# A two-layer graph kernel: the fourth pair of attention probabilities goes through DRAM too, and the steps are reordered

## The chip, the cores and the metric

One core of a Trainium2 chip. The metric is device time in microseconds (us), the median of three runs. Times inside a run are read from one profiled execution. Engines are named as the profile names them: PE is TensorE (PEld its weight loads), DVE is VectorE, ACT is ScalarE, POOL is GpSimd, SP is SyncE, whose queue issues every DMA here.

## The reference, cut to what matters

```python
# x: (64, 256, 512) f32; adj: (256, 256) 0/1
x = layernorm(x + deg*(x @ Wi.T + b) + adj @ (x @ Wj.T))            # layer 0
q, k, v = heads(x @ Wq.T + bq), heads(x @ Wk.T + bk), heads(x @ Wv.T + bv)   # 8 heads of 64
scores = where(adj == 0, -inf, q @ k.T / 8)                          # 256 x 256 for each head
out = layernorm(x + (softmax(scores) @ v) @ Wo.T + bo)               # layer 1
```

## The kernel before

The 64 graphs (batches) run one after the other, software-pipelined by hand. `steps` issues 63 steps and a `last_step`. Step b does, for batch b, scores, softmax and attention; for batch n = b + 1 the first layer and q, k, v; for batch b - 1 the output projection `y` and the last layer norm. Every product is made of three f32 products of split operands (`_hi` and `_lo` parts), so each operand costs a copy for the high part and a subtraction for the low part. The 8 heads are 4 pairs (`g` = 0 to 3, two heads `i` in each).

Every engine has its own instruction list, written out by hand in `step`, and runs it strictly in order; semaphores tie the lists together. So an instruction that waits holds back all that is listed behind it on its engine. SP's list is such a list too: a DMA whose semaphore is late holds back the DMAs behind it.

The path of one pair's probabilities: PE makes `scores` into two of the four `attn` banks; DVE `maxima_of_head` adds the mask, writes `probs` and the row minima; ACT `exponentials`; DVE `inverse_sums`; ACT `normalise_even` and POOL `normalise_odd` scale the two heads. The product with v needs them transposed. Before the change pair 0 is transposed by PE (`transpose_p`, 8 transposes of 128x128 into PSUM, L675), copied by ACT (`pt_high`) and split by DVE (`pt_low`). Pairs 1 to 3 are transposed in 32x32 blocks by DVE (`flip`, L1074) and the blocks are moved to their places by SP (`move`): one DMA of 512 KB `bounce<-probs` (L280), a wait for its landing, then four DMAs of 128 KB `pT_raw<-bounce` (L285). ACT `p_high` and DVE or POOL `p_low` split them, and PE `attend` uses them.

`probs` has two slots, g % 2. So the maxima of pair 2 may be written only when pair 0 has left slot 0, and those of pair 3 when pair 1 has left slot 1. Before, the maxima of pair 2 wait for PE's transposes (`pt_done`), those of pair 3 for `moved[1]`. Pairs run in the order 1, 0, 2, 3 (function `at`).

In each step SP's list is: `load_x` (L271), `load_xT` (512 KB, L268, which waits until PE has finished the last product of the first layer, `l0_done`), the three moves, and the store of batch b - 1.

The last layer norm is applied on DVE (`norm_apply`, L1145, two instructions of 128x512 a step).

## Time and profile before

| | |
|---|---|
| median of 3 runs | 2925.93 us (2925.61 to 2926.91) |
| the profiled execution's own time | 2926.99 us |
| its span, first to last instruction | 2925.2 us |
| PE busy | 2845.6 us, 97% |
| DVE, ACT, POOL busy | 2258.0, 1871.2, 1883.9 us |
| mean granted clock of PE | 0.996 of full |
| DMA share of 16 engines, hardware queue | 32.1% |

A step of the steady loop takes 44.80 us, so the 63 steps are nearly the whole span. Matmuls are pipelined, and their shown durations overlap: what one costs is the distance from its start to the next start. The same holds for DVE and ACT.

### The profile page before, as it was taken

What the parts mean: (1) busy time and instruction counts of PE and PEld (TensorE: products, weight loads), DVE (VectorE), ACT (ScalarE), POOL (GpSimd) and SP (SyncE); (2) the same over time, 40 slices, a digit from 0 to 9 for tenths busy, and PEclk for the clock granted to TensorE, in tenths of its full rate; (3) what the DMA queues carried; (4) which work ended last, traced back from release to release, by engine and by line L of the source; (5) the groups of instructions that cost most, each with busy time, mean ns of one, the idle gap of its engine ahead of it and who ended that gap; (6) DMA issues with size and microseconds to landing.
All of it is one profiled execution on the core that took longest, in us unless ns stands there. A gap on an engine that the chain in (4) does not pass through costs nothing.

```text
span 2925.2 us, 59805 instructions
## 1 busy us (share of the span) xinstructions
PE 2845.6 (97%) x18584; PEld 2457.2 (84%) x18584; DVE 2258.0 (77%) x5774; ACT 1871.2 (64%) x4874; POOL 1883.9 (64%) x1794
## 2 busy tenths in 40 slices
PE   6999999999999999999999999999999999999997
PEld 5888888888888888888888888888888888888886
DVE  7687777777877877778778777777787787777776
ACT  4666666666666666666666666666666666666665
POOL 5667666576676675665766766657667667666573
PEclk9999999999999999999999999999999999999999
DMA  4333333333333333333233333333333332333321
GB/s 137 109 102 102 115 100 108 108 98 111 107 100 112 103 100 110 105 108 105 96 115 102 104 110 103 105 108 103 112 101 100 115 100 100 115 100 108 107 92 60
DMA packets 282405, 306.72 MB, mean 105 GB/s; under 512 B 18817, under 2 KB 214913, under 8 KB 282369
## 3 DMA queue, kind: packets, MB, share of 16 engines
q1 hardware_dynamic: 282368, 306.26, 32.1%
q8 instruction: 19, 0.31, 0.0%
q14 instruction: 18, 0.14, 0.0%
HBM read 173.55 MB, written 132.64 MB: 105 GB/s over the span
## 4 chain that ended last, share of the span: by engine, by line
POOL 36%; issue 31%; PE 23%; DVE 7%; POOLq 1%; ACT 0%; DMA 0%; DVEq 0%; SPq 0%
PE proj L535 12%; POOL pT_lo L400 10%; POOL xb L395 5%; PE proj L498 4%; POOL probs L391 4%; POOL xs_lo L368 3%; PE attn L660 3%; POOL oT_lo L423 3%; DVE hb L1145 3%; POOL hb L409 3%; POOL mj_lo L379 2%; PE av L498 2%; POOL xs_raw L352 2%; POOL xs_raw L349 1%; DVE pT_lo L1078 1%
## 5 line engine op out<-in xcount | busy, mean ns | idle before, releaser
L400 POOL TENSOR_TENSOR pT_lo<-pT_raw,pT_hi 128x512 fp32r<-128x512 f32 x315 | 403.3, 1297 | 402.7 <-ACT pT_hi L856 402.7
L825 ACT ACTIVATE probs<-probs,row_min 128x256 f32<-128x256 f32 x1024 | 509.0, 499 | 225.5 <-DVE row_min L1043 222.9
L391 POOL TENSOR_TENSOR probs<-probs,row_inv 128x512 f32<-128x512 f32 x256 | 266.9, 1043 | 434.1 <-DVE row_inv L1054 434.1
L1043 DVE CUSTOM_DVE_ANT_0 probs<-attn,mask_add 128x256 f32<-128x256 f32 x1024 | 375.9, 418 | 41.8 <-PE attn L660 39.8
L862 ACT COPY o_part<-av 64x512 f32<-64x512 f32 x256 | 149.6, 584 | 395.1 <-PE av L498 389.1
L535 PE MATMUL proj<-wji_hi,xs_hi 128*128 128x512 f32 x896 | 363.4, 406 | 14.7 <-DVE wji_lo L1222 10.8
L535 PE MATMUL proj<-wji_hi,xs_lo 128*128 128x512 f32 x896 | 355.6, 397 | 0.0
L535 PE MATMUL proj<-wji_lo,xs_hi 128*128 128x512 f32 x896 | 355.6, 397 | 0.0
L1074 DVE STREAM_TRANSPOSE probs<-probs 128x1024 f32<-128x1024 f32 x189 | 234.7, 1242 | 114.5 <-PE av L498 114.5
L616 PE MATMUL proj<-mj_hi,wq_hi 128*128 128x256 f32 x1024 | 293.4, 286 | 11.3 <-DVE mj_lo L997 11.3
L1145 DVE TENSOR_SCALAR hb<-hb,mean_var_out,rstd_out 128x512 f32<-128x512 f32 x128 | 156.4, 1261 | 188.1 <-POOL rstd_out L418 188.0
L368 POOL TENSOR_TENSOR xs_lo<-xs_raw,xs_hi 128x768 fp32r<-128x768 f32 x126 | 295.9, 2349 | 0.2
L616 PE MATMUL proj<-mj_hi,wq_lo 128*128 128x256 f32 x1024 | 288.6, 282 | 0.0
L616 PE MATMUL proj<-mj_lo,wq_hi 128*128 128x256 f32 x1024 | 288.2, 281 | 0.0
L498 PE MATMUL av<-pT_hi,v_both 128*128 128x256 f32 x1016 | 258.7, 287 | 30.0 <-DVE pT_lo L1078 25.9
L498 PE MATMUL proj<-mj_hi,wk_lo 128*128 128x256 f32 x1024 | 287.7, 281 | 0.0
L498 PE MATMUL proj<-mj_hi,wk_hi 128*128 128x256 f32 x1024 | 287.6, 281 | 0.0
L498 PE MATMUL proj<-mj_lo,wk_hi 128*128 128x256 f32 x1024 | 287.3, 281 | 0.0
L1088 DVE SCALAR_TENSOR_TENSOR oT<-av,bv_cols,o_part 64x256 f32<-64x256 f32 x512 | 242.9, 474 | 17.0 <-ACT o_part L862 13.4
L834 ACT ACTIVATE probs<-probs,row_inv 128x256 f32<-128x256 f32 x512 | 232.1, 501 | 36.0 <-DVE row_inv L1054 36.0
L498 PE MATMUL av<-pT_lo,v_both 128*128 128x256 f32 x1016 | 252.3, 282 | 0.0
L498 PEld LDWEIGHTS av<-pT_hi,v_both 128*128 128x128 f32 x1016 | 191.2, 188 | 62.8 <-issue 53.0
(126 smaller groups left out, 8611.2 us busy)
## 6 DMA issues: line engine op xcount, KB each, us to landing
bounce<-probs SPq DMA_DIRECT2D x189, 512.0 KB, 2.6
pT_raw<-bounce SPq DMA_DIRECT2D x756, 128.0 KB, 3.0
xs_raw<-in_xT SPq DMA_DIRECT2D x64, 512.0 KB, 4.1
xb<-in_x SPq DMA_DIRECT2D x64, 512.0 KB, 3.4
out<-hb SPq DMA_DIRECT2D x64, 512.0 KB, 2.8
w_raw<-in_w0T SPq DMA_DIRECT2D x8, 256.0 KB, 5.6
stage<-in_wqT SPq DMA_DIRECT2D x1, 1024.0 KB, 10.6
stage<-in_wkT SPq DMA_DIRECT2D x1, 1024.0 KB, 12.5
```

The source lines that it names most:

```text
L368: pool.tensor_tensor(xs_lo[:, blocks, :, :], xs_raw[:, blocks, :, :], xs_hi[:, blocks.start - 1:blocks.stop - 1, :, :].bitcast(F32), ALU.s ...
L391: pool.tensor_tensor(e, e, inv, ALU.mult).then_inc(norm_odd_done, 1)
L400: pool.tensor_tensor(pT_lo[:, g % 2, :, :, i, :, :], pT_raw[:, g % 2, :, :, i, :, :], pT_hi[:, :, :, i, :, :].bitcast(F32), ALU.subtract). ...
L498: return pe.matmul(dst, lhsT, rhs, start=start, stop=stop)
L535: last = pe.matmul(proj[bank_][:, :], a[:, c, :], w[:, c, :, :].rearrange("p k o -> p (k o)"), start=(start and j == 0), stop=(j == len(te ...
L616: last = pe.matmul(dst[:, c, :], w[:, kk, cols], h[:, kk, :], start=(part == 0 and c == 0 and kk == 0 and j == 0), stop=(part == 1 and kk ...
L825: last = nc.scalar.activation(e, e, ACT.Exp, bias=row_min[:, g % 2, s:s + 1], scale=-1.0, accum_out=row_sum[:, g % 2, s:s + 1])
L834: last = nc.scalar.activation(e, e, ACT.Copy, scale=row_inv[:, g % 2, r:r + 1])
L1043: last = V.tensor_tensor_reduce(out=out_, in0=in_, in1=mask_, scale=1.0, scalar=MIN_CEILING, op0=ALU.add, op1=ALU.min, accum_out=row_min[: ...
L1074: V.transpose(both, both).then_inc(flip_done, 1)
L1088: last = V.scalar_tensor_tensor(out=oT[i * HALF:(i + 1) * HALF, g, :], in0=av[0:HALF, i * N:(i + 1) * N], scalar=bv_cols[:, 2 * g + i:2 * ...
L1145: V.tensor_scalar(row(r), row(r), mean_var[which][:, r, 0:1], rstd[which][:, r:r + 1], ALU.subtract, ALU.mult).then_inc(normed[which], 1)
```

## The change

- Pair 0 takes the path of the others: `flip`, `move`, `p_high`, `p_low`. PE's `transpose_p`, ACT's `pt_high` and DVE's `pt_low` remain only in `last_step`.
- `at` is gone: the pairs run 0, 1, 2, 3.
- The maxima of pair 2 wait for `bounced[0]`, those of pair 3 for `bounced[1]` (the landing of the DMA out of `probs`), those of pairs 0 and 1 for `bounced[2]` and `bounced[3]` of the step before.
- The last layer norm is applied on ACT (`norm_out`), from a shift that one small DVE instruction computes (`norm_shift`).
- The lists of PE, ACT, DVE and POOL are written in new orders. SP's list gets `move(b, 0)` ahead of `move(b, 1)`.

```diff
@@ SP
             def move(b, g):
-                sp.wait_ge(flip_done, 3 * b + g)
+                sp.wait_ge(flip_done, G * b + g + 1)
...
                     load_x(b + 2, parity)
                     load_xT(b + 2)
+                move(b, 0)
                 move(b, 1)
                 move(b, 2)
                 move(b, 3)
@@ PE, step
                 first_layer(n, U4)
-                transpose_p(b, 0, 0)
-                transpose_p(b, 0, 1)
                 scores(b, 1, only=2)
+                scores(b, 1, only=3)
                 aggregate(n)
                 if y_: y(b - 1, 0)
                 if y_: y(b - 1, 1)
+                transpose_h(n, 0, 1 - parity)
+                transpose_h(n, 1, 1 - parity)
                 attend(b, 0, not y_)
-                transpose_h(n, 0, 1 - parity)
-                scores(b, 1, only=3)
-                transpose_h(n, 1, 1 - parity)
                 q(n, 0)
                 q(n, 1)
                 attend(b, 1)
@@ ACT, new function
+            def norm_out(n, parity):
+                act.wait_ge(shift_done, n + 1)
+                for r in range(R):
+                    nc.scalar.activation(hb[:, parity, r, :], hb[:, parity, r, :], ACT.Identity, bias=shift[:, r:r + 1],
+                                         scale=rstd["out"][:, r:r + 1]).then_inc(normed["out"], 1)
@@ DVE, maxima_of_head
-                elif i == 0 and (g == 2 or tail and g == 3):
-
-                    dve.wait_ge(pt_done, 2 * b + 2 * (g - 2) + 2)
-                elif i == 0 and g == 3:
-
-                    dve.wait_ge(moved[1], 64 * (b + 1))
+                elif i == 0 and g >= 2:
+
+                    dve.wait_ge(bounced[g - 2], 16 * (b + 1))
+                elif i == 0 and not first:
+
+                    dve.wait_ge(bounced[g + 2], 16 * b)
@@ DVE, step, middle part
-                pt_low(b, 0, 0)
                 agg_sum(n, 1, other)
                 norm_stats("h", n, 0, read["agg"], h_row[other])
-                inverse_sums(b, 2)
                 norm_stats("h", n, 1, read["agg"], h_row[other])
                 norm_mean("h", n)
-                pt_low(b, 0, 1)
                 if y_: y_sum(b - 1, 0, other)
+                inverse_sums(b, 2)
+                maxima_of_head(b, 3, 0)
                 norm_apply("h", n, h_row[other])
+                p_low(b, 0, 0)
                 if y_: y_sum(b - 1, 1, other)
+                maxima_of_head(b, 3, 1)
+                hT_low(n, 0)
+                hT_low(n, 1)
                 flip(b, 2)
-                hT_low(n, 0)
-                maxima_of_head(b, 3, 0)
-                hT_low(n, 1)
...
-                if y_: norm_apply("out", b - 1, hb_row[other])
+                p_low(b, 2, 1)
+                if y_: norm_shift(b - 1)
                 o_sum(b, 2)
                 p_low(b, 3, 1)
@@ POOL, step
+                normalise_odd(b, 0)
                 if y_: split_o(b - 1, 3)
+                mj_low(n, 0)
                 normalise_odd(b, 1)
-                normalise_odd(b, 0)
-                mj_low(n, 0)
                mj_low(n, 1)
```

Three places in the lists, as the built programs have them. On DVE, from the flip that stands among the sums of the first layer (`mj_lo` and `xb<-proj,deg,xb` are those sums; `row_min` marks the maxima, `xb<-proj,xb` the sum of the aggregation). Before:

```order
L1074 STREAM_TRANSPOSE probs<-probs 128x1024 [waits norm_odd_done,norm_even_done,av_done]
L1106 TENSOR_TENSOR mj_lo<-proj,mj_hi 128x256 [waits mj_hi_done,l0_done]
L1114 SCALAR_TENSOR_TENSOR xb<-proj,deg,xb 128x256
L1043 ISA probs,row_min<-attn,mask_add 128x8x32 [waits score_done,pt_done]
L1043 ISA row_min 128x1
```

After:

```order
L1072 STREAM_TRANSPOSE probs<-probs 128x1024 [waits norm_odd_done,norm_even_done,av_done]
L1054 RECIPROCAL row_inv<-row_sum 128x4 [waits exp_done]
L1104 TENSOR_TENSOR mj_lo<-proj,mj_hi 128x256 [waits mj_hi_done,l0_done]
L1112 SCALAR_TENSOR_TENSOR xb<-proj,deg,xb 128x256
L1072 STREAM_TRANSPOSE probs<-probs 128x1024 [waits norm_odd_done,norm_even_done,av_done]
L1043 ISA probs,row_min<-attn,mask_add 128x8x32 [waits score_done,bounced0]
L1043 ISA row_min 128x1
```

Pair 0 is flipped at the place where pair 1 was, pair 1 follows, and the maxima of pair 2 stand behind both with a wait for a DMA. Further down DVE's list, from the applied first layer norm (`xb<-xb,mean_var_h,rstd_h`) to the low part of its transpose (`mj_lo<-proj,mj_hi 128x512`, which PE's q waits for). Before:

```order
L1145 TENSOR_SCALAR xb<-xb,mean_var_h,rstd_h 128x512 [waits rstd_h_done]
L1145 TENSOR_SCALAR xb<-xb,mean_var_h,rstd_h 128x512
L1126 TENSOR_TENSOR hb<-proj,hb 128x512 [waits hb_ready,y_done]
L1074 STREAM_TRANSPOSE probs<-probs 128x1024 [waits norm_odd_done,norm_even_done,av_done]
L997 TENSOR_TENSOR mj_lo<-proj,mj_hi 128x512 [waits hT_hi_done]
```

After, from the maxima of pair 3:

```order
L1043 ISA probs,row_min<-attn,mask_add 128x8x32 [waits score_done,bounced1]
L1043 ISA row_min 128x1
L1043 ISA probs,row_min<-attn,mask_add 128x8x32
L1043 ISA row_min 128x1
L1152 TENSOR_SCALAR xb<-xb,mean_var_h,rstd_h 128x512 [waits rstd_h_done]
L1152 TENSOR_SCALAR xb<-xb,mean_var_h,rstd_h 128x512
L1076 TENSOR_TENSOR pT_lo<-pT_raw,pT_hi 128x8x64 [waits p_hi_done]
L1124 TENSOR_TENSOR hb<-proj,hb 128x512 [waits hb_ready,y_done]
L1043 ISA probs,row_min<-attn,mask_add 128x8x32 [waits score_done]
```

The maxima of pair 3 and their wait now stand ahead of the applied norm, and four more instructions stand between it and the low part. On SP, from the load of the transposed x. Before:

```order
L268 DMA xs_raw<-in_xT 128x1024 [waits l0_done]
L280 DMA bounce<-probs 128x1024 [waits flip_done]
L285 DMA pT_raw<-bounce 32x8x128 [waits bounced1]
L285 DMA pT_raw<-bounce 32x8x128 x3
L280 DMA bounce<-probs 128x1024 [waits flip_done]
L285 DMA pT_raw<-bounce 32x8x128 [waits bounced2]
```

After:

```order
L267 DMA xs_raw<-in_xT 128x1024 [waits l0_done]
L279 DMA bounce<-probs 128x1024 [waits flip_done]
L284 DMA pT_raw<-bounce 32x8x128 [waits bounced0]
L284 DMA pT_raw<-bounce 32x8x128 x3
L279 DMA bounce<-probs 128x1024 [waits flip_done]
L284 DMA pT_raw<-bounce 32x8x128 [waits bounced1]
```

The DMA out of pair 1's slot is now the second one, behind the four DMAs of pair 0.

## Rows read from the trace of the kernel before

**Rows 1.** The page: span, busy time by engine, one group of section 5.

```profile
span 2925.2 us, 59805 instructions
...
PE 2845.6 (97%) x18584; PEld 2457.2 (84%) x18584; DVE 2258.0 (77%) x5774; ACT 1871.2 (64%) x4874; POOL 1883.9 (64%) x1794
...
L1145 DVE TENSOR_SCALAR hb<-hb,mean_var_out,rstd_out 128x512 f32<-128x512 f32 x128 | 156.4, 1261 | 188.1 <-POOL rstd_out L418 188.0
```

**Rows 2.** Windows, one step: us; busy PE, PEld, DVE, ACT, POOL; PEclk; DMA; GB/s.

```profile
1405.26:1450.06 44.80, 44.21 (x293) 38.25 (x292) 34.83 (x89) 29.02 (x76) 29.39 (x29) 1.00 0.32 105
```

**Rows 3.** Waits of TensorE, whole span: total us, times, longest us.

```profile
PE av L498 <- DVE pT_lo L1078: 25.9, 63, 0.4
PE proj L616 <- DVE mj_lo L997: 11.3, 63, 0.6
...
PE proj L588 <- DVE xb L1145: 5.1, 1, 5.1
```

**Rows 4.** Timeline, TensorE, that step: start us, us, engine, line, operation, count, [idle].

```profile
1405.26 0.39 PE L660 MATMUL attn<-k_hi,q_hi 64*128 64x256 f32 x2
...
1406.88 0.50 PE L535 MATMUL proj<-wji_hi,xs_hi 128*128 128x512 f32 x1
...
1416.78 1.03 PE L675 MATMUL attn<-ident,probs 128*128 128x128 f32 x8
1417.74 0.39 PE L660 MATMUL attn<-k_hi,q_hi 64*128 64x256 f32 x2
...
1418.65 0.73 PE L498 MATMUL proj<-mj_hi,aT 128*128 128x512 f32 x2
...
1429.42 0.36 PE L616 MATMUL proj<-mj_hi,wq_hi 128*128 128x256 f32 x1 [0.17 <-DVE mj_lo L997]
```


**Rows 5.** The same timeline, the end of that step.

```profile
1450.06 0.39 PE L660 MATMUL attn<-k_hi,q_hi 64*128 64x256 f32 x2
```

**Rows 6.** Timeline of SyncE's queue, the same step.

```profile
1416.97 0.36 SPq L268 DMA_DIRECT2D xs_raw<-in_xT  x1
1417.57 0.34 SPq L280 DMA_DIRECT2D bounce<-probs  x1
1422.26 2.55 SPq L285 DMA_DIRECT2D pT_raw<-bounce  x4
1428.63 0.34 SPq L280 DMA_DIRECT2D bounce<-probs  x1
1431.27 2.54 SPq L285 DMA_DIRECT2D pT_raw<-bounce  x4
```

**Rows 7.** Timeline of SyncE's queue, a step that loads no x.

```profile
2850.33 0.33 SPq L280 DMA_DIRECT2D bounce<-probs  x1
2852.97 2.54 SPq L285 DMA_DIRECT2D pT_raw<-bounce  x4
```

**Rows 8.** Timeline of VectorE, the same step as rows 4.

```profile
1416.31 1.24 DVE L1074 STREAM_TRANSPOSE probs<-probs 128x1024 f32<-128x1024 f32 x1
...
1424.66 0.68 DVE L1126 TENSOR_TENSOR hb<-proj,hb 128x512 f32<-128x512 f32 x1
1425.33 1.00 DVE L1145 TENSOR_SCALAR xb<-xb,mean_var_h,rstd_h 128x512 f32<-128x512 f32 x2
1426.41 0.69 DVE L1126 TENSOR_TENSOR hb<-proj,hb 128x512 f32<-128x512 f32 x1
...
1428.58 0.69 DVE L997 TENSOR_TENSOR mj_lo<-proj,mj_hi 128x512 fp32r<-128x512 f32 x1
1429.19 0.41 DVE L1043 CUSTOM_DVE_ANT_0 probs<-attn,mask_add 128x256 f32<-128x256 f32 x1
...
1429.90 0.69 DVE L997 TENSOR_TENSOR mj_lo<-proj,mj_hi 128x512 fp32r<-128x512 f32 x1
...
1447.51 1.26 DVE L1078 TENSOR_TENSOR pT_lo<-pT_raw,pT_hi 128x512 fp32r<-128x512 f32 x1
```

**Rows 9.** Windows as rows 2, a stretch of the first step.

```profile
80.00:86.00 6.00, 5.36 (x29) 4.84 (x30) 4.14 (x9) 1.17 (x2) 0.97 (x3) 0.50 0.49 162
```

More of the change, by code:

```diff
@@ L215, in build @@
         flip_done, p_hi_done = sem("flip_done"), sem("p_hi_done")
-        moved = {g: sem(f"moved{g}") for g in (1, 2, 3)}
-        bounced = {g: sem(f"bounced{g}") for g in (1, 2, 3)}
-        p_split = {g: sem(f"p_split{g}") for g in (1, 2, 3)}
+        moved = [sem(f"moved{g}") for g in range(G)]
+        bounced = [sem(f"bounced{g}") for g in range(G)]
+        p_split = [sem(f"p_split{g}") for g in range(G)]
         stats_done = {k: sem(f"stats_{k}_done") for k in ("h", "out")}
@@ L640, in scores @@
                 pe.wait_ge(read["k"], 2 * b + pair + 1)
-                pairs = ((only,) if only is not None else (0, 1) if last else (1, 0))
+                pairs = (0, 1) if only is None else (only,)
                 if tail:
-                    pe.wait_ge(pt_read, 2 * b + 2 * (only - 2) + 2)
+                    pe.wait_ge(pt_read, 2 * (only - 2) + 2)
                 elif pair == 0 and not first:
                     pe.wait_ge(max_done, 2 * G * b)
-                elif only == 2:
-                    pe.wait_ge(max_done, 2 * (G * b + at(0)) + 2)
-                elif only == 3:
-                    pe.wait_ge(pt_read, 2 * b + 2)
+                elif only is not None:
+                    pe.wait_ge(max_done, 2 * (G * b + only - 2) + 2)
                 for g in pairs:
@@ L1136, in norm_mean @@
             def norm_mean(which, n):
+                if which == "out" and not (type(n) is int and n == 0):
+                    dve.wait_ge(normed["out"], R * n)
+                    dve.nop(nofuse=True)
                 dve.wait_ge(stats_done[which], R * n + R)
@@ L1325, in last_step @@
                 maxima(b, 3, tail=True)
+                o_sum(b, 1)
+                pt_low(b, 2, 0)
+                pt_low(b, 2, 1)
                 inverse_sums(b, 3, tail=True)
[L1327 to L1330 removed]
                 norm_mean("out", b - 1)
                 o_sum(b, 2)
[L1333 removed]
+                pt_low(b, 3, 0)
+                pt_low(b, 3, 1)
+                norm_shift(b - 1)
                 o_sum(b, 3)
[L1335 removed]
             steps(dve, step, last_step)
```

210 lines of the change are left out of this document (103 added, 107 removed).

## The prediction

> **What bounds the kernel now.** The page first: PE is busy for 97% of the span [rows 1]. Then one step of the loop, cut out as a window from the start of one `scores` to the next: 44.80 us, with PE at work for 44.21, DVE for 34.83, ACT for 29.02, POOL for 29.39, the clock at 1.00 and the DMA engines at 0.32 [rows 2]. Then the waits of PE: over the whole span it waits only in two places of the loop, 25.9 us for the low part of the last pair and 11.3 us for the low part of `hT`, 0.6 us a step together [rows 3]. So PE's own list is the bound, and the other engines have spare time in the mean. Spare time in the mean is not enough, though. Every other list is in order, and the chain that feeds PE's `q` may become later than PE. So I follow one step, on a clock that is 0 at the start of its first scores, 1405.26 in the trace. On that clock, before: the first layer starts at 1.62, the transposes at 11.52, scores of pair 2 at 12.48, the aggregation at 13.39, `q` at 24.16, and the next step at 44.80 [rows 4, 5]. From the start of `q` to the end of the step are 20.64 us.
>
> **What PE saves.** The 8 transposes occupy 11.52 to 12.48, 0.96 us. Two pairs of scores in one go take 1.62 us (0 to 1.62), one pair alone 0.91 us (12.48 to 13.39), so that putting pairs 2 and 3 together saves 2 x 0.91 - 1.62 = 0.20 us. Together 1.16 us a step, 73 us over 63 steps. The wait for the last pair's low part stays: it hangs on `p_high(b, 3)`, which waits for `attend(b, 2)`, as before.
>
> **What the other engines gain and lose.** DVE loses the second layer norm (2 x 1.26 us [rows 1]) and two `pt_low` (0.7 each, estimated from the equal shape of `mj_lo`, 0.69), and gains a flip (1.24) and two `p_low` (1.26 each) [rows 8]: 3.9 out, 3.8 in, so its 34.83 us stay. ACT gains two applications of 128x512. The rows have no such instruction on it; between nothing and DVE's 1.26 I take the high end, 2.5 us, which its 15.8 idle us a step hide, since the store that waits for them is needed only a step later. If that cover were gone it would cost up to 2.5. POOL has the same work in another order; its `mj_low(n, 1)` now waits behind `normalise_odd(b, 1)` and comes some 0.5 us late for the aggregation, which is swallowed by the larger wait below. DMA traffic of the moves rises by a third, from a share of 0.32 of the whole: room enough. None of this decides.
>
> **The new waits.** DVE's flip among the sums of the first layer starts at 11.05 and takes 1.24, so it is done at 12.3, just where SP issues the first bounce (12.31) [rows 6, 8]. After the change the same set of DVE work (four maxima, two `v_low`, one `o_sum`, the sums) stands ahead of that flip, so `flip(b, 0)` is done at the same time. Nor could an earlier one help: SP must first issue `xs_raw<-in_xT`, which waits for the end of the first layer and goes out at 11.71 [rows 6]. From there:
>
> 1. The first bounce is issued at 12.31 and the four DMAs behind its landing start at 17.00: 4.69 us, not the 2.63 us that a bounce takes later in the step (23.37 to 26.01) [rows 6]. The reason is the x load 0.60 us ahead of it: in a step without that load the first bounce takes 2.64 us [rows 7]. The maxima of pair 2, which before waited for PE's transposes, now wait for this landing. DVE stands still from about 14.7 (the first flip's end at 12.3, a sum of some 0.8 and a second flip of 1.24, with a short wait between) to 17.0, and the aggregation's sums, which free PE's bank for the second half of `y`, stand behind it.
> 2. SP needs 2.55 us to issue the four DMAs of pair 0 [rows 6], so that the bounce of pair 1, though flipped at 14.7, goes out at 19.6.
> 3. How long that bounce takes behind four DMAs of 128 KB, the trace doesn't show. Alone it is 2.63, behind 512 KB issued 0.6 us earlier 4.69. The four are the same 512 KB, but issued over 2.55 us, so most of it has moved by then: I take 3.3, nearer to the low end. It lands at 22.9.
> 4. The maxima of pair 3 wait for it, and behind them in DVE's list stand: head 0 of those maxima 0.71, the applied norm of the first layer 1.08, `p_low(b, 0, 0)` 1.26, `y_sum` 0.67, head 1 of the maxima 0.71, `hT_low` 0.69 (each as the distance between starts, or the duration, in [rows 8]), and 0.15 from the end of that to the start of `q` (1429.27 to 1429.42 [rows 4, 8]). Sum 5.27 us.
>
> So `q` starts at 22.9 + 5.27 = 28.2 in place of 24.16, 4.0 us late, although PE has less to do ahead of it. What is late next is the whole rest of the step: with 20.64 us behind it the step becomes 48.8 us. PE's waits then lie ahead of `transpose_h` (from about 22 to 24.7), and ahead of `q` (about 1 us), since `transpose_h` and `attend(b, 0)` are short.
>
> Is anything else late in the 20.64? Pair 1's reloads are issued by 25.5 and, with a landing as long as a bounce's, are there at 28.1. ACT reaches `p_high(b, 1)` only at about 30, after the exponentials of pair 3, and POOL's two halves, which I take as long as DVE's `p_low`, end at some 33.1. `attend(b, 1)` is due behind `q`, whose 48 products take some 5.8 us, at 33.9 or so. These three are estimates by the counting above. That is close but holds. Pairs 2 and 3 have more room.
>
> **The sum.** 61 full steps x 4.0 = 244 us. The step that loads no x gets its first bounce 2.05 us sooner: 2.0. The first step, which has no `y` and already waits 5.1 us for the applied norm [rows 3], I put at 3. The last step keeps PE's transposes: nothing. Together 249 us on the profiled execution's own 2926.99 us, which is 1.1 us above the median: 3176 us. With step 3 at its two ends (2.63 and 4.69) the step is 48.1 or 50.2 us, and the time 3135 or 3262: this case's own range.
>
> Of the bounce behind other DMAs the Trainium skill says (DMA: Bandwidth & Descriptors, Queues, rings and completion order) that each DMA engine takes its descriptors in ring order. By that rule the second bounce would move nothing until pair 0's reloads are through, nearer to 3.8 us than to 3.3, and the sum would be some 30 us more. The trace agrees in so far as the bounce behind the x load takes 2.05 us more than the one alone.
>
> **The rivals.**
>
> *The clock falls in the new waits.* Once in the trace PE waits 5.1 us, in the first step and for this same applied norm, and right behind it the granted clock is 0.50 from 80 to 86 us [rows 3, 9]; such a stretch of at least 6 us costs half its work, 3 us. In the changed steps PE would stand some 2.7 us and then 1 us. That is less than 5.1 at one go, so it needn't fall, and it may fall in some steps only. If it falls in a third of them: 21 x 3 = 63 us more, 3240 us; in all of them 3365 us. The Trainium skill (TensorE: Matmul & The Clock Gate, Why this matters for your kernels) warns of idle gaps of PE between bursts for this reason. By that rule the slower figures are the likelier ones; the trace shows only the one long wait.
>
> *The DMAs don't hold each other up.* If both bounces took 2.63 us, pair 0 would land at 14.95 and pair 1 at 20.2. `q` would start at 25.5, 1.3 us late, and the kernel would take 2927 + 63 x 1.3 = 3009 us. Against it stands that 4.69 us is what each step with an x load shows.
>
> *The other side: faster.* DVE's chain behind the second bounce needs 5.27 us and `q` must start by 24.16, so the change breaks even if that bounce lands by 18.9, and wins if it lands earlier. With no new wait at all PE's saving remains: 2927 - 73 = 2854 us. For it speaks that PE is the only engine near full [rows 2]. Against it, the bounce isn't issued before 19.6 by rows 6. It would need SP to issue the reloads faster, or a first bounce that doesn't feel the x load, and both together.
>
> **How the numbers follow.** Chances: the chain as worked out, clock up, 0.48; the same with the clock falling in some steps, 0.33 (0.04 of it above 3290); the milder one 0.09; the faster one 0.07; and 0.03 for a time within 0.2% (about 6 us, what a measurement of this kernel can tell from no change), where savings and waits cancel by chance. The likeliest gives 3176 us. The range from 3080 to 3290 leaves out the milder, the faster and the worst clock cases, 0.2 together or a little more. Faster 0.07, same 0.03, slower 0.90.
>
> **What would show it in the profile after.** In SP's queue: the first bounce 4.7 us ahead of its four reloads, the second bounce right behind them, and about 3.3 us to its landing. In the waits: DVE's maxima (L1043) waiting some 2 us a step for `bounce`, and PE waiting for `xb` ahead of `transpose_h` and for `mj_lo` ahead of `q`, 3 to 4 us a step together, where before it waited 0.2. The step at 48.8 us. PE's busy time down by some 60 us or more. The clock column in the windows behind those waits tells the first rival. The prediction is wrong if the first bounce lands by 15, or if DVE reaches the first flip much sooner than 11 and that turns out to matter, or if another engine's list (POOL behind pair 1's low parts is the closest) ends later than `attend(b, 1)`.

## The result, and the profile after

The changed kernel takes 3358.74 us (median of 4 runs, 3356.73 to 3359.12), the one before 2926.42 beside it: a ratio of 1.1476, 95% interval 1.1456 to 1.1496. That is 432 us slower, and 69 us above the upper end of the forecast range. The page after, to be read against [rows 1]:

```profile
span 3357.3 us, 59354 instructions
PE 2924.1 (87%) x18080; PEld 2481.4 (74%) x18080; DVE 2393.1 (71%) x5774; ACT 1966.4 (59%) x5000; POOL 1939.6 (58%) x1794
```

PE no longer fills its span. Its busy time did not fall by the transposes' worth; it rose by 78 us, and part of it ran at half clock (mean clock 0.958 of full, before 0.996). What PE waits for (against [rows 3]; total us, times, longest):

```profile
PE proj L588 <- DVE xb L1152: 251.4, 64, 10.0
PE av L498 <- DVE pT_lo L1076: 85.8, 63, 1.4
PE proj L498 <- DVE xb L1118: 49.1, 61, 1.0
```

And what DVE waits for. The first row is pair 2's maxima standing for the landing of pair 0's DMA to DRAM. The second names no releaser; in the step below it is pair 3's maxima, which start 0.10 us behind the issue of the reloads that wait for pair 1's landing:

```profile
DVE probs L1043 <- DMA bounce<-probs: 161.4, 63, 2.8
...
DVE probs L1043 <- issue: 81.0, 63, 2.0
```

The step of after that is read here starts at 1041.48 and lasts 51.58 us (the mean over all steps is 51.65, before 44.78). SP's queue in it (start, us), to be read against [rows 6]:

```profile
1053.39 0.35 SPq L267 DMA_DIRECT2D xs_raw<-in_xT  x1
1053.88 0.34 SPq L279 DMA_DIRECT2D bounce<-probs  x1
1058.86 2.56 SPq L284 DMA_DIRECT2D pT_raw<-bounce  x4
1061.53 0.53 SPq L279 DMA_DIRECT2D bounce<-probs  x1
1065.03 2.53 SPq L284 DMA_DIRECT2D pT_raw<-bounce  x4
```

The first trip takes 4.98 us, the second, behind the four reloads, 3.50. DVE and POOL behind the second landing (against [rows 8]):

```profile
1052.54 1.24 DVE L1072 STREAM_TRANSPOSE probs<-probs 128x1024 f32<-128x1024 f32 x1
...
1058.98 0.42 DVE L1043 CUSTOM_DVE_ANT_0 probs<-attn,mask_add 128x256 f32<-128x256 f32 x1 [2.65 <-DMA bounce<-probs]
...
1065.13 0.42 DVE L1043 CUSTOM_DVE_ANT_0 probs<-attn,mask_add 128x256 f32<-128x256 f32 x1 [1.21 <-issue]
...
1065.83 2.07 DVE L1152 TENSOR_SCALAR xb<-xb,mean_var_h,rstd_h 128x512 f32<-128x512 f32 x2
```

```profile
1065.18 1.27 POOL L400 TENSOR_TENSOR pT_lo<-pT_raw,pT_hi 128x512 fp32r<-128x512 f32 x1 [0.94 <-ACT pT_hi L849]
1066.40 1.22 POOL L391 TENSOR_TENSOR probs<-probs,row_inv 128x512 f32<-128x512 f32 x1
```

The applied norm, 1.00 us for its two instructions before, takes 2.07 here, while POOL works on SBUF at the same time. PE stands 3.79 us for it:

```profile
1061.10 0.50 PE L498 MATMUL proj<-wo_hi,oT_hi 128*128 128x512 f32 x1 [0.84 <-DVE xb L1118]
1067.96 1.97 PE L588 MATMUL proj<-ident,xb 128*128 128x128 f32 x8 [3.79 <-DVE xb L1152]
```

Behind that wait the granted clock is at its lower level (0.50, 1.2 GHz), while the transposes of `h` and pair 0's product run (windows: from:to, us, busy us of PE, PEld, DVE, ACT, POOL, clock, DMA share, GB/s):

```profile
1060.00:1067.00 7.00, 3.33 (x14) 2.17 (x12) 5.69 (x18) 3.21 (x10) 2.72 (x4) 1.00 0.53 162
...
1068.00:1070.00 2.00, 2.00 (x10) 2.00 (x11) 2.00 (x7) 0.89 (x2) 1.93 (x3) 0.50 0.48 128
1070.00:1071.00 1.00, 1.00 (x7) 1.00 (x7) 0.42 (x1) 0.98 (x3) 0.92 (x2) 0.60 0.00 0
1071.00:1076.00 5.00, 5.00 (x44) 5.00 (x43) 2.82 (x5) 4.61 (x14) 1.77 (x3) 1.00 0.26 105
```

So `q` starts at 29.68 on the step's clock, not at 24.16 as before or at 28.2 as forecast. From `q` to the end it takes 21.90 us, not 20.64. This second loss has its own place. DVE's shift for the last norm, a mere 128x2, lasts until POOL's `x_low` is done, and ACT's `norm_out` waits 3.15 us for it with `o_part` and `p_high` of the last pairs queued behind:

```profile
1085.40 1.79 DVE L1146 SCALAR_TENSOR_TENSOR shift<-mean_var_out,rstd_out 128x2 f32<-128x2 f32 x1 [0.87 <-POOL rstd_out L418]
```

```profile
1085.34 1.84 POOL L368 TENSOR_TENSOR xs_lo<-xs_raw,xs_hi 128x768 fp32r<-128x768 f32 x1
```

```profile
1087.23 1.52 ACT L854 ACTIVATE hb<-hb,shift,rstd_out 128x512 f32<-128x512 f32 x2 [3.15 <-DVE shift L1146]
1088.78 0.58 ACT L861 COPY o_part<-av 64x512 f32<-64x512 f32 x1
1089.26 1.14 ACT L849 CAST pT_hi<-pT_raw 128x512 fp32r<-128x512 f32 x2
```

PE's wait ahead of pair 3's product is 1.4 us a step for it (85.8 in all), where it was 0.4.

Two theories go to the chip. **A:** three separate losses add up: DVE's list standing for the DRAM landings, the clock behind PE's long wait, and the norm's move, whose shift stands behind POOL. **B**, the rival: one loss (the DRAM trip of pair 0) sets the step, and the others lie beside it.

### The profile page after: what moved, and what is told of

Read it like the earlier page. It is cut to its first block, busy times and chain, and to the rows that moved or that the text cites. A ratio compares the mean times of both kernels' runs of the same rounds, so it can differ in the third digit from the quotient of the medians.

```text
span 3357.3 us, 59354 instructions
## 1 busy us (share of the span) xinstructions
PE 2924.1 (87%) x18080; PEld 2481.4 (74%) x18080; DVE 2393.1 (71%) x5774; ACT 1966.4 (59%) x5000; POOL 1939.6 (58%) x1794
## 4 chain that ended last, share of the span: by engine, by line
PE 60%; DMA 14%; DVE 8%; issue 6%; SPq 5%; ACT 5%; POOL 1%; DVEq 0%; POOLq 0%; ACTq 0%
PE proj L535 19%; PE proj L498 17%; DMA bounce<-probs 14%; PE proj L616 10%; PE av L498 9%; SPq L284 5%; DVE xb L1152 4%; PE attn L657 3%; DVE pT_lo L1076 3%; PE proj L588 2%; ACT pT_hi L849 2%; ACT hb L854 1%; ACT o_part L861 1%; DVE probs L1043 1%; SPq L267 1%
## 5 line engine op out<-in xcount | busy, mean ns | idle before, releaser
L1072 DVE STREAM_TRANSPOSE probs<-probs 128x1024 f32<-128x1024 f32 x252 | 312.7, 1241 | 133.7 <-PE av L498 108.4
L498 PE MATMUL av<-pT_hi,v_both 128*128 128x256 f32 x1016 | 309.7, 330 | 90.0 <-DVE pT_lo L1076 85.8
L849 ACT CAST pT_hi<-pT_raw 128x512 fp32r<-128x512 f32 x504 | 286.2, 617 | 91.1 <-DMA pT_raw<-bounce 91.1
L423 POOL TENSOR_TENSOR oT_lo<-oT,oT_hi 128x256 fp32r<-128x256 f32 x256 | 184.2, 741 | 264.5 <-ACT oT_hi L868 264.5
L588 PE MATMUL proj<-ident,xb 128*128 128x128 f32 x512 | 100.0, 358 | 251.4 <-DVE xb L1152 251.4
L498 PEld LDWEIGHTS av<-pT_hi,v_both 128*128 128x128 f32 x1016 | 224.6, 221 | 123.2 <-issue 105.7
L616 PE MATMUL proj<-mj_hi,wq_hi 128*128 128x256 f32 x1024 | 308.0, 301 | 0.8 <-DVE mj_lo L997 0.6
L616 PE MATMUL proj<-mj_hi,wq_lo 128*128 128x256 f32 x1024 | 303.6, 297 | 0.0
L616 PE MATMUL proj<-mj_lo,wq_hi 128*128 128x256 f32 x1024 | 301.2, 294 | 0.0
L498 PE MATMUL av<-pT_lo,v_both 128*128 128x256 f32 x1016 | 292.2, 313 | 0.0
## 6 DMA issues: line engine op xcount, KB each, us to landing
stage<-in_wkT SPq DMA_DIRECT2D x1, 1024.0 KB, 12.4
```

The lines of the kernel that those rows point to most:

```text
L423: pool.tensor_tensor(oT_lo[:, g, :], oT[:, g, :], oT_hi[:, g, :].bitcast(F32), ALU.subtract).then_inc(o_split, 1)
L498: return pe.matmul(dst, lhsT, rhs, start=start, stop=stop)
L616: last = pe.matmul(dst[:, c, :], w[:, kk, cols], h[:, kk, :], start=(part == 0 and c == 0 and kk == 0 and j == 0), stop=(part == 1 and kk ...
L849: nc.scalar.copy(pT_hi[:, :, :, i, :, :], pT_raw[:, g % 2, :, :, i, :, :]).then_inc(p_hi_done, 1)
L1072: V.transpose(both, both).then_inc(flip_done, 1)
```

## The experiments

All ratios are to the kernel before, with 95% intervals; "less" is against the changed kernel's 3358.74 us. Numbers 7, 10, 11 and 15 edit the kernel before, all others the changed one. Where a run's diff is shown against another run, the line above it says so.

### 1. x's transposed load behind the bounces

```diff
@@ SP
-                    load_xT(b + 2)
                 move(b, 0)
                 move(b, 1)
+                if ahead:
+                    load_xT(b + 2)
```

> The changed kernel with one edit in SP's list: the load of the transposed x stands behind the moves of pairs 0 and 1 in place of ahead of them. Theory (each step hangs on the landing of the second bounce): the first bounce lands in about 2.6 us in place of 4.9, the second is issued 2.3 us sooner and lands near 3.5 us after its issue, PE's wait for xb shrinks from 3.8 us a step to under 1.5, so that the clock no longer falls there; 2.4 to 3.5 us a step less, 3140 to 3210 us. Rival (the second bounce is not what the step hangs on, or the later load makes POOL's sums late in its place): within 40 us of the changed kernel's 3359 us.

3225.39 us, 1.1016 (1.0998 to 1.1035), 133 us less. The first bounce takes 2.63 us (median), so the load ahead of it cost the other 2.3. The wait for the applied norm falls from 251.4 to 168.5 us. In return GpSimd now waits 257.3 us for the later load. The time is 15 us above the theory's range, and far from the rival's.

### 2. PE kept busy through its long wait

```diff
+            def keep_busy(b, first):
+                if not first:
+                    pe.wait_ge(av_read, G * b)
+                for i in range(14):
+                    mm(av[:, :], w_hi["wo"][:, i % C, 0:P], w_hi["wo"][:, i % C, :], True, True)
...
+                keep_busy(b, not y_)
                 transpose_h(n, 0, 1 - parity)
```

> The changed kernel with 14 extra products of 128x512 on PE in each step, between y and transpose_h, into the av bank, which nobody reads before attend overwrites it; they fill the wait of PE without ending later than it. Theory 1 (the fallen clock is most of what the prediction missed, about 2 us a step): 3230 to 3270 us. Theory 2 (VectorE's chain to the low part of hT is nearly as late as PE is, so the fallen clock costs only what PE is later than it, 0.6 us a step, and more only where the clock stays low longer): 3290 to 3325 us. Theory 3 (no cost of the clock at all): 3350 us or more.

3301.74 us, 1.1275 (1.1257 to 1.1294), mean clock 0.994 instead of 0.958. The clock is thus worth 57 us in this kernel, 0.9 us a step, and not the 3 us of my rival. DVE's chain is nearly as late as PE at half clock: with PE kept busy, 32.8 us of new waits stand ahead of `q` for the low part of `hT`.

### 3. Pair 3's maxima behind the chain to `q`

```diff
-                maxima_of_head(b, 3, 0)
                 norm_apply("h", n, h_row[other])
                 p_low(b, 0, 0)
                 if y_: y_sum(b - 1, 1, other)
-                maxima_of_head(b, 3, 1)
                 hT_low(n, 0)
+                maxima_of_head(b, 3, 0)
                 hT_low(n, 1)
+                maxima_of_head(b, 3, 1)
```

> The changed kernel with the two maxima of pair 3 moved down VectorE's list, behind the applied norm, p_low of pair 0, y_sum and the first low part of hT (where the kernel before has them). Nothing else changes; SP's order stays. Theory (the wait for the second bounce holds back the applied norm): the norm is applied about 2 us sooner, and one of the maxima no longer stands ahead of hT's low part, together 2.5 to 3.5 us a step, and PE's wait becomes too short for the clock to fall: 3130 to 3200 us. Rival (the chain hangs on the first bounce and the sums behind it alone): less than 1 us a step, 3300 us or more.

3220.77 us, 1.0999 (1.0981 to 1.1018), 138 us less, again some 20 us above the theory's range. The long wait (now 84.3 us) was mostly that of DVE's list and not of the data: nothing in the chain to `q` needs the second landing. The mean clock is 0.991 here instead of 0.958, so the 138 us hold most of what the clock cost, too.

```profile
PE av L498 <- DVE pT_lo L1076: 85.7, 63, 1.4
PE proj L588 <- DVE xb L1152: 84.3, 63, 7.6
PE proj L498 <- DVE xb L1118: 48.9, 61, 2.7
PE av L498 <- POOL pT_lo L400: 48.2, 52, 1.2
```

### 4. The last norm back on DVE

```diff
-                if y_: norm_out(b - 1, 1 - parity)
...
-                if y_: norm_shift(b - 1)
+                if y_: norm_apply("out", b - 1, hb_row[other])
```

> The changed kernel with the last layer norm applied on VectorE again, at the place where the shift is computed. Theory (ScalarE waits for the shift in front of o_low_part and p_high of the last pairs, which costs PE's attend(b, 3) about 0.9 us a step): 3290 to 3310 us. Rival (that wait is covered, or the norm's 2.5 us on VectorE make p_low(b, 3, 1) just as late): 3350 us or more.

3349.41 us, 1.1437 (1.1418 to 1.1456): only 9 us less, as the rival had it. At its new place the norm costs as much on DVE. POOL runs `x_low` and `add_bias` at that time, and its two instructions took 4.62 us in the step read, from 1442.92.

### 5 and 6. POOL held back, and the norm's output later

```diff
@@ 5: POOL
                 root("h", n)
+                pool.wait_ge(normed["h"], R * (n + 1))
                 p_low(b, 0, 1)
@@ 6: ACT
-                if y_: norm_out(b - 1, 1 - parity)
                 o_low_part(b, 2)
                 p_high(b, 3)
+                if y_: norm_out(b - 1, 1 - parity)
```

> The changed kernel with one wait more on POOL: ahead of p_low(b, 0, 1) it waits until VectorE has applied the first layer's norm. So POOL works on nothing while VectorE applies it. Theory (VectorE's two instructions of 128x512 take 2.0 us there in place of 1.0 because POOL works in SBUF at the same time): their time falls to 1.0 to 1.1 us a step, transpose_h starts 0.9 us sooner, and the kernel takes 3290 to 3310 us, if the clock falls as often as now; less if it falls more seldom. Rival (the two instructions are slow for another reason, or the late p_low makes attend(b, 0) late instead): 3345 us or more.

> The changed kernel with norm_out moved behind o_low_part(b, 2) and p_high(b, 3) on ScalarE. Theory (ScalarE stands in front of them waiting for a shift that VectorE delivers only when POOL's x_low is through, and this makes PE's wait in attend(b, 3) 1.4 us a step in place of 0.4): that wait falls to 0.4 to 0.5 us, 3290 to 3310 us. Rival, from the run with the norm on VectorE (only 9 us gained, the same 81 us of that wait): the wait has another cause, and the kernel takes 3340 us or more.

The first takes 3326.6 us, 1.136 (1.1341 to 1.1379), the second 3330.89, 1.1382 (1.1363 to 1.1401): 32 and 28 us less, both short of what theory A expected. With POOL held, the applied norm takes 542 ns an instruction instead of 1073, over all steps (first the changed kernel, then this one):

```profile
L1152 DVE TENSOR_SCALAR xb<-xb,mean_var_h,rstd_h 128x512 f32<-128x512 f32 x128 | 132.4, 1073 | 1.1 <-POOL rstd_h L418 1.1
```

```profile
L1153 DVE TENSOR_SCALAR xb<-xb,mean_var_h,rstd_h 128x512 f32<-128x512 f32 x128 | 63.9, 542 | 1.2 <-POOL rstd_h L418 1.2
```

So what slowed it was POOL's work beside it. The wait for it falls by 68 us, but pair 0's second low part comes later (24.7 us of new wait ahead of pair 0's product). With the norm later, PE waits 52.1 us for POOL's low part of pair 3 in place of 85.8 for DVE's. Each of the two waits had the cause that was named, and something stood close behind it.

### 7. The norm's move alone, on the kernel before

```diff
@@ ACT
                 k_high(n, 1)
+                if y_: norm_out(b - 1, 1 - parity)
                 o_low_part(b, 2)
@@ DVE
-                if y_: norm_apply("out", b - 1, hb_row[other])
+                if y_: norm_shift(b - 1)
```

> The kernel before with one part of the change alone: the last norm applied on ScalarE, with norm_shift at the place of the applied norm on VectorE, and norm_out ahead of o_low_part(b, 2) on ScalarE. Theory (the small shift instruction waits on VectorE until POOL's x_low is through, and ScalarE behind it): attend(b, 3) waits 1.4 us a step in place of 0.4, so 2975 to 3005 us. Rival (the move is free, as the prediction had it): 2920 to 2935 us.

3112.84 us, 1.0637 (1.0619 to 1.0655). Both expectations missed: one instruction of 128x2 and two on an idle engine cost 186 us. PE waits 2.1 us a step ahead of pair 3's product, and the clock falls behind that wait. In the step read the wait ends at 1441.20; the first window below reaches from inside the wait to the clock's return, the two others lie behind it:

```profile
PE av L500 <- DVE pT_lo L1087: 128.6, 63, 2.1
```

```profile
1440.00:1446.00 6.00, 4.80 (x34) 4.37 (x35) 4.14 (x11) 1.85 (x4) 6.00 (x6) 0.72 0.09 33
...
1442.00:1443.00 1.00, 1.00 (x7) 0.78 (x5) 0.00 (x0) 0.00 (x0) 1.00 (x1) 0.50 0.00 0
...
1444.00:1445.00 1.00, 1.00 (x14) 1.00 (x12) 0.98 (x3) 0.82 (x2) 1.00 (x2) 0.50 0.00 0
```

### 8. All that stands behind a landing moved

`load_xT` as in 1, POOL's wait as in 5, DVE's maxima as in 3, and besides:

```diff
@@ ACT
-                exponentials(b, 3)
                 p_high(b, 1)
+                exponentials(b, 3)
                 q_high(n, 0)
-                if ahead: x_high(b + 2, 0)
...
-                k_high(n, 0)
                 p_high(b, 2)
-                if ahead: x_high(b + 2, 1)
                 if y_: norm_out(b - 1, 1 - parity)
+                k_high(n, 0)
+                if ahead: x_high(b + 2, 0)
+                if ahead: x_high(b + 2, 1)
@@ DVE
                 o_sum(b, 0, not y_)
+                if y_: norm_stats("out", b - 1, 0, read["y"], hb_row[other])
                 q_low(n, 0)
+                if y_: norm_stats("out", b - 1, 1, read["y"], hb_row[other])
+                if y_: norm_mean("out", b - 1)
...
                 o_sum(b, 1)
-                if y_: norm_stats("out", b - 1, 0, read["y"], hb_row[other])
-                if y_: norm_stats("out", b - 1, 1, read["y"], hb_row[other])
+                if y_: norm_shift(b - 1)
                 q_low(n, 1)
-                if y_: norm_mean("out", b - 1)
                 k_low_half(n, 0)
                 p_low(b, 2, 1)
-                if y_: norm_shift(b - 1)
@@ POOL
                 normalise_odd(b, 2)
-                if ahead: sum_x(b + 2)
...
                 normalise_odd(b, 3)
-                p_low(b, 2, 0)
                 if y_: root("out", b - 1)
-                if ahead: x_low(b + 2, 0)
+                if ahead: sum_x(b + 2)
+                p_low(b, 2, 0)
                 if ahead: add_bias(b + 2, parity)
+                if ahead: x_low(b + 2, 0)
```

> The changed kernel with its way of moving all four pairs kept and the orders mended: the x load behind the moves of pairs 0 and 1; the maxima of pair 3 behind the applied norm; POOL holding until that norm is applied; p_high of pair 1 ahead of the exponentials of pair 3; the statistics, root and shift of the last norm earlier and norm_out ahead of k_high; sum_x behind pair 1's low parts. Theory (all of the loss is in these orders, and PE's 1.16 us a step are then won): q starts 24 us into the step, the step is 43.9 to 44.9 us, 2870 to 2935 us. Rival (the two DMA legs of pair 0 cannot be hidden in any order like this one): a step of 46 us or more, 3000 us or more.

3106.1 us, 1.061 (1.0593 to 1.0628), far from the 2870 to 2935 of the theory; the number is the rival's, but not for its reason. `q` now starts at 24.2 on the step's clock, as in the kernel before. Up to there the DRAM way costs no more than the 1.16 us that PE no longer spends. The rest takes 23.3 us. More than half of what it has over the 20.64 of before is DVE's low part of pair 2 beside POOL's `add_bias`: in two steps read it took 1.87 and 2.46 us, and pair 2's product came 1.46 and 2.06 us late.

### 9. The tail mended too

Against run 8:

```diff
@@ DVE
                 if y_: norm_stats("out", b - 1, 0, read["y"], hb_row[other])
-                q_low(n, 0)
                 if y_: norm_stats("out", b - 1, 1, read["y"], hb_row[other])
                 if y_: norm_mean("out", b - 1)
                 inverse_sums(b, 3)
+                q_low(n, 0)
                 flip(b, 3)
-                o_sum(b, 1)
                 if y_: norm_shift(b - 1)
+                o_sum(b, 1)
...
-                p_low(b, 2, 1)
@@ POOL
                 p_low(b, 2, 0)
+                p_low(b, 2, 1)
@@ ACT
-                if y_: norm_out(b - 1, 1 - parity)
                 k_high(n, 0)
+                if y_: norm_out(b - 1, 1 - parity)
```

> The kernel with all steps moved up, plus: the norm's shift stands behind the last flip of the step and not ahead of it, both low parts of pair 2 are GpSimd's, the statistics of the new residual come ahead of q's low half, and k's first high half stands ahead of the norm's output on ScalarE. Theory: what that kernel still lost lay in the tail of the step, in TensorE's waits for low parts that VectorE writes beside GpSimd (0.70, 1.20, 0.40 and 0.68 us a step), and the transposes by way of DRAM cost nothing once they are asked for early enough: a step of 44.5 to 45.2 us, 2900 to 2950 us. Rival: the way by DRAM itself takes something that no order gives back; then the time stays at 3000 us or more.

2958.97 us, 1.0101 (1.0073 to 1.0129). 400 of the 432 us are back with all four pairs still going by DRAM and the norm still on ACT. The theory's range ended at 2950 us, so what is left was not expected.

### 10. The kernel of 7, PE kept busy

```diff
                 v(n, 1)
+                pe.wait_ge(max_done, 2 * G * (b + 1))
+                for i in range(7):
+                    mm(attn[0][:, :], w_hi["wo"][:, i % C, 0:P], w_hi["wo"][:, i % C, :], True, True)
                 attend(b, 3)
```

> The kernel before with its last norm on ScalarE alone, and 7 dummy products of 128x512 on TensorE into a free bank, ahead of the last pair's product with v, in the 2.1 us in which it otherwise stands waiting for that pair's low part. Their results are overwritten. Theory 1: about half of the 3.0 us a step that this kernel loses is the clock that falls to 1.2 GHz behind that wait; then the time is 3020 to 3040 us (the wait itself stays, at 1.7 us over the old one, or 1.4 to 1.8 us a step). Theory 2: the wait for VectorE's chain is all of it, and the clock's fall lies beside it; then 3100 us or more.

3032.34 us, 1.0357 (1.0339 to 1.0374), mean clock 0.994 instead of 0.965. Theory 1: of the 186 us of kernel 7, 81 are the clock and 105 the wait.

### 11. The kernel of 7, POOL free

```diff
@@ POOL
-                if ahead: x_low(b + 2, 0)
                 p_low(b, 3, 0)
+                if ahead: x_low(b + 2, 0)
```

> The kernel before with its last norm on ScalarE alone, and on GpSimd the low part of x stands behind the low part of the last pair and not ahead of it, so that GpSimd runs nothing long when VectorE comes to the norm's shift. Theory 1: the shift, 128 rows of 2, takes 1.78 us only because it stands until GpSimd's running instruction ends; then it takes under 0.2 us here, the wait ahead of the last pair's product with v goes back to about 0.4 us, and the time to 2925 to 2950 us. Theory 2: the shift is late whatever GpSimd does, since ScalarE's two norm instructions (1.5 us) push the o part and p's high half back by themselves; then 3050 us or more.

2933.2 us, 1.0021 (1.0011 to 1.003). Swapping two POOL instructions takes back 180 of 186 us, and theory 2 (3050 us or more) is out. The swap also lets POOL's own low part of pair 3 go sooner; but it is DVE's low part for which PE waited in kernel 7. The group of the shift, first in kernel 7, then here (busy us, mean ns):

```profile
L1157 DVE SCALAR_TENSOR_TENSOR shift<-mean_var_out,rstd_out 128x2 f32<-128x2 f32 x62 | 108.9, 1757 | 186.9 <-POOL rstd_out L420 186.9
```

```profile
L1157 DVE SCALAR_TENSOR_TENSOR shift<-mean_var_out,rstd_out 128x2 f32<-128x2 f32 x62 | 10.0, 161 | 186.6 <-POOL rstd_out L420 186.6
```

1757 ns against 161 for the same instruction: it stands until POOL's running instruction ends. In the rows of the changed kernel above, the shift ends at 1087.19 and POOL's `x_low` at 1087.18. The Trainium skill states this (SBUF — State Buffer, Who interferes with whom): a DVE instruction with two SBUF inputs, or a `tensor_scalar` in a two-port mode, and a GpSimd instruction that reads SBUF exclude each other for the whole instruction. The traces agree here with the shift, and with the applied norm (1.00, 2.07 and 4.62 us), though no run here shows in which mode the norm runs.

### 12. The mended order of 9, norm on DVE

Against run 9:

```diff
@@ ACT
-                if y_: norm_out(b - 1, 1 - parity)
@@ DVE
-                if y_: norm_shift(b - 1)
...
                 k_low_half(n, 0)
+                if y_: norm_apply("out", b - 1, hb_row[other])
```

> The mended order (all four pairs by DRAM) with the last norm applied on VectorE, behind k's low half, instead of on ScalarE. It tells the transposes alone from the norm's move. Theory: the transposes by way of DRAM are worth about the 1 us a step that TensorE no longer spends on pair 0, less what the DRAM trip takes; with the norm back, 2900 to 2960 us, near the kernel with the same order and the norm on ScalarE. Rival: the norm on VectorE lengthens the chain to q or the tail as it did in the kernel of the change, and the time is 3000 us or more.

2970.45 us, 1.0146 (1.0129 to 1.0163). In this order the norm on ACT saves 11 us; the DRAM way alone, with the norm on DVE, is 1.5% slower than the kernel before, 10 us above the range that was expected.

### 13 to 18. Is the last 1% the order's or the DRAM way's?

```diff
@@ 13 on 9, and 15 on the kernel before: ACT, DVE
-                o_low_part(b, 2)
                 p_high(b, 3)
+                o_low_part(b, 2)
...
-                o_sum(b, 2)
                 p_low(b, 3, 1)
+                o_sum(b, 2)
@@ 17 on 9, 14 on 13: DVE (p_low(b, 0, 1) leaves POOL)
                 p_low(b, 0, 0)
-                if y_: y_sum(b - 1, 1, other)
+                p_low(b, 0, 1)
                 hT_low(n, 0)
-                maxima_of_head(b, 3, 0)
+                if y_: y_sum(b - 1, 1, other)
                 hT_low(n, 1)
+                maxima_of_head(b, 3, 0)
@@ 18 on 17, 16 on 14: POOL
-                if ahead: x_low(b + 2, 0)
                 p_low(b, 3, 0)
+                if ahead: x_low(b + 2, 0)
```

> The mended kernel (2959 us) with pair 3's high part ahead of pair 2's output part on ScalarE, and its low part ahead of pair 2's output sum on VectorE. Theory: the wait of 0.52 us ahead of pair 3's product goes, nothing else moves: 2925 to 2940 us. Rival: the time that is left comes from the DRAM legs, and the wait turns up elsewhere: 2950 us or more.

> The kernel with pair 3 ahead, and pair 0's second low part on VectorE (0.68 us there) instead of on GpSimd (1.56 us beside it), with the second half of y's sum behind the first half of h's low part. Theory: the wait of 0.69 us ahead of pair 0's product goes too, 30 to 40 us more: 2885 to 2910 us, so that the way by DRAM is then faster than the kernel before (2927 us). Rival: what stands behind it on VectorE (y's sum, the last pair's maxima) makes TensorE wait as long: 2920 us or more.

> The kernel before, with pair 3's high and low part ahead of pair 2's output part and sum, in the same two places. Its trace has a wait of 0.41 us a step there. Theory: that wait goes, and 20 to 26 us with it: 2900 to 2907 us. Rival: VectorE's other work behind it (pair 2's output sum, k's low half) then comes late and costs the same: 2920 us or more.

> The kernel with both of these orders mended, and GpSimd's low part of x (1.9 us) behind pair 3's low part and not ahead of it. Theory: GpSimd then is free when pair 3's high part is there, and VectorE's subtraction beside it has no one to wait for: 0 to 15 us less than that kernel. Rival: x's low part, 0.8 us later or more, holds the next first layer or the residual's sum back: 10 us more.

> The mended kernel (2959 us) with pair 0's second low part on VectorE and the second half of y's sum behind the first half of h's low part; pair 3 as it was. Theory: TensorE's wait ahead of pair 0's product falls from 0.69 to 0.19 us a step, and 0.2 us come in for y's bank: 15 to 35 us less, 2924 to 2944 us, within 0.6% of the kernel before. Rival: what is left is the DRAM way's and the time stays at 2950 us or more.

> The same, with GpSimd's low part of x behind pair 3's low part. Theory: 0 to 12 us less than the kernel without that move, since the low parts of pair 3 and of pair 2 then never stand behind it; 2915 to 2940 us. Rival: x's low part comes too late for the next first layer, and the time is above the other's.

| run | us | ratio (95%) |
|---|---|---|
| 13 | 2997.54 | 1.0226 (1.0209 to 1.0244) |
| 14 | 3014.96 | 1.0288 (1.0271 to 1.0305) |
| 15 | 2954.03 | 1.0091 (1.0074 to 1.0108) |
| 16 | 3006.11 | 1.027 (1.0252 to 1.0288) |
| 17 | 2978.71 | 1.0188 (1.0163 to 1.0212) |
| 18 | 2954.24 | 1.0087 (1.007 to 1.0104) |

Only 16, 9 us below 14, came out as its theory had it. 13, 14, 15 and 17 are slower than the kernels that they edit, where each was to be faster. 18 gains 25 us on 17, but stays above its range of 2915 to 2940.

Pair 3's move ahead was a mistake of mine: its product writes the bank that `o_sum(b, 2)` still has to read. In 15 the wait doubles from 25.9 us and changes its name:

```profile
PE av L498 <- DVE oT L1088: 51.6, 63, 1.3
```

In 14 and 17 pair 0's wait falls as expected (from 43.0 to 11.7 and 10.6 us), but others open: 17 is 20 us slower than 9, with 36.0 us of waits for POOL's low parts. 18 takes those away and equals 9 within the spread of the two kernels' runs. None of these beats the kernel before.

Where PE's time goes is seen when the distances between the starts of its stages are laid side by side, one step of each kernel (us; each stage with the wait behind it; after is the step from 1402.40, 18 the one from 1417.83):

| stage | before | after | 18 |
|---|---|---|---|
| scores 0, 1 | 1.62 | 1.63 | 1.63 |
| first layer | 9.90 | 10.16 | 10.17 |
| transposes of pair 0, scores 2 (after: scores 2, 3) | 1.87 | 1.63 | 1.62 |
| aggregation | 1.97 | 2.38 | 2.38 |
| `y` | 5.59 | 10.67 | 5.62 |
| `h` transposed, pair 0's product (before: scores 3) | 3.21 | 3.21 | 2.66 |
| `q` to pair 2's product | 16.12 | 16.46 | 16.13 |
| `v`, row 1 | 3.37 | 4.34 | 3.53 |
| pair 3's product | 1.15 | 1.15 | 1.14 |
| step | 44.80 | 51.63 | 44.88 |

PE drops 0.96 us of transposes and 0.20 of scores, as worked out. But in both new kernels the first layer takes 0.26 to 0.27 more and the aggregation 0.41: PE gets there earlier than the sums of the other engines. For the aggregation the trace of after shows it: its second row of products starts 0.05 us behind the end of POOL's low part.

```profile
1054.91 1.30 POOL L379 TENSOR_TENSOR mj_lo<-mj_raw,mj_hi 128x512 fp32r<-128x512 f32 x1
```

```profile
1056.26 0.73 PE L498 MATMUL proj<-mj_hi,aT 128*128 128x512 f32 x2
```

In 18, pair 0's product and its wait take 1.41 us instead of 0.94. The saving is eaten within the step. The step read for 18 is a short one: the distances between the stores give a mean of 45.07 us in 18 and 44.78 before. So the table shows where the waits lie, not all that they come to.

## Why the prediction was wrong

The direction and the first place were right: `q` is late, and behind the second landing. The size was not: 3359 us measured, 3176 forecast. Each step is 51.65 us instead of 48.8, and 63 times the 2.85 us of difference is 180 of the 183 us. Two steps of the working failed. Up to `q` it is a term of the sum, the applied norm at 1.08 us, which took 2.00. Behind `q` it is a term put at nothing, the norm's move to ACT, behind which the 20.64 us became 21.90. Of the 2.8 us a step, 1.5 lie ahead of `q` and 1.3 behind it.

- **PE's saving (1.16 us):** the instructions went away as worked out, but 0.67 of it came back as waits in the first layer and the aggregation. The aggregation's I had named (`mj_low(n, 1)` some 0.5 us late), the first layer's not. Neither is part of the 183 us, for the sum did not count on the saving; they matter in the mended kernels.
- **The flip and the first bounce:** right to 0.1 us in place (1053.88 is 12.4 on the step's clock, 12.31 forecast); the landing is 4.98 behind instead of 4.69.
- **"I take 3.3" for the second bounce:** measured 3.50 (median 3.51), between the 3.3 and the 3.8 of the ring-order reading. With the first it puts the landing at 23.55 instead of 22.9: 0.65 us of the miss.
- **The chain of 5.27 us behind it:** 6.13 measured. The failed term is the applied norm, "1.08", which took 2.00 between starts, for POOL's `p_low` and `normalise_odd` now lie beside it (run 5: 1.00 with POOL held). `p_low(b, 0, 0)` went the other way, 0.60 instead of 1.26: the row of before that I read lay beside one of POOL's. And PE at half clock brought `q` 0.6 us later than its data. The other terms held to 0.1. The trace of before held the warning: the pair of norm instructions takes 1.00 us for `h`, and 2.51 for the last norm, beside POOL's `x_low`:

```profile
1444.02 1.84 POOL L368 TENSOR_TENSOR xs_lo<-xs_raw,xs_hi 128x768 fp32r<-128x768 f32 x1
```

```profile
1444.09 2.51 DVE L1145 TENSOR_SCALAR hb<-hb,mean_var_out,rstd_out 128x512 f32<-128x512 f32 x2 [3.04 <-POOL rstd_out L418]
```

- **The clock rival:** I gave it a third of the steps at 3 us each. The clock falls all along: windows of 500 us each show 0.96 or 0.97. But it is worth only 0.9 us a step (run 2); in the step read it is low only to about 1071, over few products, and DVE is late beside it. I had also read the trace of before wrongly. It has two long waits of PE, and the stretch at half clock that I put behind the 5.1 us (80 to 86) stands behind the other one, of 4.02 us for pair 0's low part. The half clock behind the 5.1 us is from 40 on:

```profile
39.96 1.97 PE L588 MATMUL proj<-ident,xb 128*128 128x128 f32 x8 [5.15 <-DVE xb L1145]
...
80.64 0.55 PE L498 MATMUL av<-pT_hi,v_both 128*128 128x256 f32 x1 [4.02 <-DVE pT_lo L1060]
```

```profile
40.00:46.00 6.00, 5.36 (x25) 4.99 (x26) 5.14 (x5) 1.17 (x2) 5.80 (x5) 0.52 0.49 177
```

So "less than 5.1 at one go, so it needn't fall" compared with the wrong row; it fell behind 3.79 us in the changed kernel and behind 2.10 us in run 7.

- **"ACT's idle time hides" the norm's two instructions:** this step failed outright. `norm_out` itself was short (1.52 us for both). What I did not cost was what stands behind it in ACT's list, and that its shift on DVE waits for POOL. I said the wait ahead of pair 3's product stays as before; it grew by 1.0 us a step, and the time from `q` to the end by 1.26. Run 11 shows the mechanism on the kernel before. In the changed kernel no single run took the whole 1.26 away: runs 4 and 6 gained 9 and 28 us, since in run 4 the norm holds DVE instead, and in run 6 POOL's low part is nearly as late.
- **"Pair 1 is close but holds":** it held, in the changed kernel.

Of the theories, A is borne out in that there are three causes, each with a run that moves it: DVE's list (3), the clock (2), the norm's move (7, 10 and 11). It is not borne out in that they add up. The single edits gave 133, 138, 57, 32 and 28 us, but they overlap, as run 3's clock shows, and run 8, with most of them and more moved, gave back 253 us. That they come to 388, near the 400 of run 9, proves nothing. B fails on runs 3 and 8: the DRAM trip of pair 0 set the step only through the order of DVE's list. What stays open is the last 1% or so (26 to 43 us in 9, 12 and 18). The stage table places some of it in small waits of PE, but no order I ran removed them all, and whether some order could was not shown.

## What to carry over

An instruction that waits for a landing holds all that stands behind it in its engine's list, so a new wait is priced by what is queued there, and one cure is a place further down (138 us here). When work moves to an idle engine, look at what runs at that moment on DVE and on POOL together, and at the list behind it; idle time in the mean pays for nothing. Work taken off the busiest engine ahead of a point that others feed can turn into a wait at that point; here 0.67 of 1.16 us did.

## What the runs showed of the hardware

- A DVE instruction of 128x2 took 1757 ns beside one POOL instruction and 161 ns without it (runs 7, 11). Two `tensor_scalar` of 128x512 took 1.00 us with POOL idle (run 5), 2.07 in the changed kernel and 4.62 in run 4, by what POOL was doing.
- Behind a wait of PE of 2.10 us (run 7, the step read) the granted clock was 0.50, the level of 1.2 GHz, in the windows from 1442 to 1445; the low clock cost that kernel 81 us in the whole (run 10). Behind a wait of 1.39 us ahead of the same product in the changed kernel (at 1091.91) the windows read show 1.00.
- A bounce, from its issue to that of the first reload, takes 2.63 us alone (run 1), 3.5 behind four reloads issued over 2.5 us (the changed kernel), and 4.8 (before, median) to 4.9 (after) behind the x load issued 0.5 to 0.6 us earlier.
- ACT normalises two tiles of 128x512 in 1.52 us (the changed kernel, 1087.23), against 1.00 on DVE with POOL idle (run 5).
